# Depthwise convolution and two bias additions: from TensorE's matmuls to VectorE's passes

## The chip, the cores and the metric

The kernel runs on one core of one Trainium2 chip. The metric is the device time of one execution in microseconds (us), the median of three runs. Engines are named as in the profile: PE is TensorE's matmul and PEld its weight load, DVE is VectorE, ACT is ScalarE, POOL is GpSimd, SP is SyncE.

## The reference

Eight images of 56 x 56 positions with 128 channels, float32, go through two layers. The part that the change touches, cut to its lines:

```python
# x: [8, 56, 56, 128]
xp = x @ w_in + b_in
h = conv3x3_depthwise(x, dw_w) + dw_b            # feature_group_count = C
h = (h - bn_m) * (bn_g / sqrt(bn_v + 1e-05)) + bn_b
h = gelu(h)
offset = (h @ w_off + b_off).reshape(N, H, W, GROUP, P, 2)          # P = 9 samples
mask = softmax((h @ w_msk + b_msk).reshape(N, H, W, GROUP, P))
y = dcn_core(xp, offset, mask) @ w_out + b_out   # bilinear samples at the offsets, weighted
x = x + gamma1 * layer_norm(y, ln1_g, ln1_b)
m = gelu(x @ w_fc1 + b_fc1) @ w_fc2 + b_fc2
x = x + gamma2 * layer_norm(m, ln2_g, ln2_b)
```

Behind it comes layer 1: an additive attention (for every pair of positions the tanh of a sum of two 16-vectors, scored, exponentiated, masked to earlier positions and summed over the normalized x), then a routed feed-forward with 64 experts that each choose 8 positions of an image.

## The kernel before

An image is cut three ways: into 7 bands of 8 rows (448 positions), into 49 subs of 64 positions, and into 25 blocks of 128 positions (the last has 64). Channels or positions lie on the 128 partitions.

For each **band**, step `image_in` transposes x on PE and DVE copies it into the zero-bordered image `x_pad` (channels on partitions). `project_in` makes xp, and 27 steps `patches` write 2 x 2 patches of xp to HBM. `conv` is the depthwise convolution of the band: nine PE matmuls with the diagonal matrices `taps`, one for each tap, into the bank `side_ps`; ACT applies batch norm and gelu from `side_ps` into `h_band` (L1653). `offsets` multiplies `h_band` by the offset and mask weights (14 small matmuls, L1788), and DVE turns the result into gather indices (L1310 and what follows, about fifteen instructions); `weights` makes the corner weights after ACT's exp of the mask.

For each **sub**, POOL issues 18 indirect DMAs (L1189) that gather the patches into one of four slots of `gathered`. It may do so when DVE has finished the sub that used the slot before. DVE's step `sample` multiplies the gathered patches by the weights in six passes (L1372) and sums them into `y` (L1375). I call the 18 gathers of a sub a **burst**.

For each **block** follows the chain `turn`, `mix`, `turn_mid`, `hidden`, `mlp_out`, `turn_norm`, `keys`: PE and DVE (for `hidden` ACT) take turns on the one bank `chain_ps`. `mix` is the output projection, `mlp_out` the MLP's second layer; the biases of both are added by a matmul of a row of ones with the bias row (L1799, L1820), and both end in DVE's `add_norm`. Then the attention: ACT makes `unit` (tanh, L1677), PE `score` (L1846), ACT `exp` (L1687), PE and DVE `values` (L1746, L1441, L1875), DVE `finish`; `route` and `logits` prepare layer 1's second half. PE's matmuls of float32 stand in the trace as two records each.

**What sets the order.** Each engine runs one fixed list of steps. `list_schedule` makes it in Python when the kernel is built: from due times (`due_times`), needs (`needs`) and assumed durations (`LASTS`) it places the steps of many images until they repeat, and `order_of` gives the period that the loop over pairs of images repeats; `first_order` and `last_order` make the lists ahead of and behind the loop. An engine that waits for a semaphore therefore holds up all that stands behind in its list. All steps in `SIDE` share the one PSUM bank `side_ps`; PE begins one when the reader of the one before has signalled.

## Time and profile before

| what | value |
|---|---|
| median of three runs | 15282.85 us (15266.24 to 15287.42) |
| profiled execution, its own time | 15399.26 us |
| its span, first to last instruction | 15397.4 us |
| busy PE, PEld | 7675.1 us (50%), 3859.4 us (25%) |
| busy DVE, ACT, POOL | 5935.6 us (39%), 6773.1 us (44%), 6700.8 us (44%) |
| mean granted TensorE clock | 0.697 of full speed |

Span and time of the profiled execution differ by 1.9 us; it is 0.76% longer than the median of the plain runs. Busy shares are means over the whole span; none is near 100%, so what bounds the kernel has to be read from waits. POOL's last gather ends at 14967.99 us; ahead of it the span is eight images with one and the same rhythm, behind it the rest of the last image.

### The profile page before, as it was taken

The page shows a single profiled execution, that of the slowest core. Times are in us where ns is not written, and L with a number is a line of the kernel's source. Part 1 is how long each engine was busy: PE and PEld are TensorE (multiplying, and loading weights), DVE is VectorE, ACT ScalarE, POOL GpSimd, SP SyncE. Part 2 cuts the span into 40 slices and gives each one's busy share as a digit, 9 for nine tenths or more (in the row PEclk, how much of TensorE's full clock was granted, in tenths as well). Part 3 has the DMA queues.
Part 4 walks back from the last instruction along what each step waited for, and adds up shares of the span by engine and source line. Part 5 has one row for each costly group of instructions (what it writes and reads, how often), then busy time and mean ns, then how long its engine had stood idle before and what let it go on. Part 6 is the DMA issues. An engine that isn't in the chain of part 4 may idle for free.

```text
span 15397.4 us, 152662 instructions
## 1 busy us (share of the span) xinstructions
PE 7675.1 (50%) x45913; PEld 3859.4 (25%) x45913; DVE 5935.6 (39%) x17381; ACT 6773.1 (44%) x8210; POOL 6700.8 (44%) x7060
## 2 busy tenths in 40 slices
PE   3344554455534555445554455444654445544467
PEld 2122222222222222222222222222222222222234
DVE  3333334333343334333334333443333433343343
ACT  1234642455424554245533455334553355523455
POOL 4444444444444344444444444444444444444430
PEclk6566776677766776667766777666776677766778
DMA  2111111111111111111111111111111111212324
GB/s 61 45 46 34 31 42 44 45 33 34 40 46 41 31 36 42 47 39 32 38 40 46 39 32 37 43 46 37 31 40 41 48 35 33 57 55 62 94 69 158
DMA packets 453794, 711.94 MB, mean 46 GB/s; under 512 B 146561, under 2 KB 260994, under 8 KB 451330
## 3 DMA queue, kind: packets, MB, share of 16 engines
q0 software_dynamic: 225792, 462.87, 11.3%
q1 hardware_dynamic: 227170, 239.11, 4.9%
q8 instruction: 384, 6.29, 0.2%
q14 instruction: 448, 3.67, 0.1%
HBM read 595.45 MB, written 105.96 MB: 46 GB/s over the span
## 4 chain that ended last, share of the span: by engine, by line
another core or an unknown queue 36%; ACT 16%; PE 16%; issue 14%; DVE 12%; DVEq 5%; DMA 1%; SPq 0%; POOL 0%; ACTq 0%; POOLq 0%
ACT tanh L1677 13%; PE score_ps L1846 7%; DVEq L1208 5%; DVE pool_mem L1372 2%; PE value_ps L1875 2%; DVE newton L1243 2%; PE side_ps L1777 1%; DVE rstd L1245 1%; PE turn_ps L1746 1%; PE chain_ps L1814 1%; ACT expo L1687 1%; DVE bst L1250 1%; ACT L1687 1%; PE chain_ps L1822 1%
## 5 line engine op out<-in xcount | busy, mean ns | idle before, releaser
L1677 ACT ACTIVATE tanh<-key_rep,query 128x896 f32<-128x896 f32 (+7 forms) x6400 | 5560.0, 950 | 5834.7 <-remote 3382.9
L1189 POOL DMA_INDIRECT pool_mem<-patches_even,pool_mem x3528 | 3350.3, 950 | 4142.1 <-DVE y L1375 3038.2
L1189 POOL DMA_INDIRECT pool_mem<-patches_odd,pool_mem x3528 | 3350.3, 950 | 4124.9 <-DVE y L1375 3100.9
L1846 PE MATMUL score_ps<-tanh,score_w 128*32 128x512 f32 (+3 forms) x24320 | 3703.9, 650 | 2566.8 <-ACT tanh L1677 1562.2
L1846 PEld LDWEIGHTS score_ps<-tanh,score_w 128*32 128x32 f32 x24320 | 855.6, 126 | 4803.6 <-issue 2891.3
L1875 PE MATMUL value_ps<-values,expoT 128*128 128x129 f32 (+1 forms) x5200 | 1019.9, 346 | 301.0 <-issue 194.6
L1372 DVE TENSOR_TENSOR pool_mem<-pool_mem 128x384 f32<-128x384 f32 x2352 | 1136.1, 552 | 47.7 <-issue 45.5
L1375 DVE TENSOR_REDUCE y<-pool_mem 128x64 f32<-128x2304 f32 x392 | 1000.9, 2553 | 36.0 <-issue 6.7
L1875 PEld LDWEIGHTS value_ps<-values,expoT 128*128 128x128 f32 (+1 forms) x5200 | 898.6, 249 | 423.2 <-issue 300.9
L1441 DVE COPY expoT<-turn_ps 128x512 f32<-128x512 f32 (+4 forms) x800 | 456.9, 572 | 1214.5 <-remote 829.0
L1746 PE MATMUL turn_ps<-ident,expo 128*128 128x128 f32 (+1 forms) x2632 | 572.9, 341 | 682.6 <-DVE expoT L1441 510.4
L1687 ACT ACTIVATE expo<-score_ps,tiny 128x896 f32<-128x896 f32 (+9 forms) x416 | 383.4, 922 | 897.1 <-remote 599.8
L1243 DVE SCALAR_TENSOR_TENSOR newton<-rstd,newton 128x1 f32<-128x1 f32 (+1 forms) x2403 | 528.3, 220 | 211.4 <-issue 34.9
L1746 PEld LDWEIGHTS turn_ps<-ident,expo 128*128 128x128 f32 (+1 forms) x2632 | 393.8, 178 | 822.9 <-DVE expoT L1441 452.5
L1250 DVE BATCH_NORM_STATS2 bst<-chain_ps 128x6 f32<-128x128 f32 (+1 forms) x400 | 118.3, 296 | 1231.6 <-remote 721.2
L1814 PE MATMUL chain_ps<-chainT,w_fc 128*128 128x128 f32 (+1 forms) x1600 | 338.6, 379 | 501.1 <-DVE chainT L1394 418.8
L1687 ACT ACT_TABLE_LOAD x197 | 252.8, 1283 | 760.1 <-remote 686.3
L1831 PE MATMUL chain_ps<-chainT,w_key 128*128 128x128 f32 (+1 forms) x400 | 140.4, 450 | 843.5 <-DVE chainT L1410 563.8
L1777 PE MATMUL side_ps<-pool_mem,early 128*128 128x448 f32 x1008 | 427.5, 581 | 108.1 <-DVEq L1208 107.0
L1245 DVE SCALAR_TENSOR_TENSOR rstd<-newton,rstd 128x1 f32<-128x1 f32 (+1 forms) x2403 | 385.7, 161 | 222.0 <-issue 31.8
L1394 DVE COPY chainT<-chain_ps 128x128 f32<-128x128 f32 (+1 forms) x200 | 57.3, 287 | 1070.0 <-remote 894.4
L1814 PEld LDWEIGHTS chain_ps<-chainT,w_fc 128*128 128x128 f32 x1600 | 300.8, 280 | 599.2 <-DVE chainT L1394 459.9
(170 smaller groups left out, 6557.5 us busy)
## 6 DMA issues: line engine op xcount, KB each, us to landing
pool_mem<-in_weight SPq DMA_DIRECT2D x64, 1024.0 KB, 9.1
pool_mem<-patches_even,pool_mem POOLq DMA_INDIRECT x3528
pool_mem<-patches_odd,pool_mem POOLq DMA_INDIRECT x3528
patches_even<-pool_mem SPq DMA_DIRECT2D x104, 256.0 KB, 2.0
patches_odd<-pool_mem SPq DMA_DIRECT2D x104, 256.0 KB
pool_mem<-in_x SPq DMA_DIRECT2D x56, 224.0 KB
x_tok<-in_x SPq DMA_DIRECT2D x192, 64.0 KB
x_d<-x SPq DMA_DIRECT2D x192, 64.0 KB
```

The costliest lines, as they stand in the source:

```text
L1189: pool.indirect_dma_start(gathered[:, b, j * 4 * CG:(j + 1) * 4 * CG], None, patches_flat[int(odd)], bass.IndirectOffsetOnAxis(ap=index[:, ...
L1208: return v.drain()
L1243: v.scalar_tensor_tensor(newton[:r, 1:2], rstd[:r], rstd[:r], newton[:r, 0:1], ALU.mult, ALU.mult)
L1372: v.tensor_tensor(part, part, weight[:, lo:lo + PIECE].unsqueeze(2) .to_broadcast([P, PIECE, CG, 4]), ALU.mult)
L1375: v.tensor_reduce(y[:, i // 2 % 2, b].rearrange("p (g c) -> p g c", c=CG), product.rearrange("p (g t) c k -> p g c t k", g=2), AX_XY, ALU. ...
L1677: nc.scalar.activation(tanh[:, ui % TANH_SLOTS, :w], key_rep[:, lo:lo + w], ACT.Tanh, bias=query[:, col:col + 1]).then_inc(tanh_done.sem, 1)
L1687: nc.scalar.activation(expo[:r, ci % 2, :w], score_ps[:r, ci % 2, :w], ACT.Exp, bias=tiny[:r, 2:3])\
L1746: return mm(out, src, ident[:r, :r], is_transpose=True, start=True, stop=True)
L1777: last = mm(side_ps[:, :BAND], taps[:, t], x_pad[:, i * BAND_ROWS + dy:(i + 1) * BAND_ROWS + dy, dx:dx + W], start=t == 0, stop=t == TAPS - 1)
L1814: last = mm(chain_ps[:, c * P:c * P + r], w_fc1[:, c * P:(c + 1) * P], chainT[:, :r], start=True, stop=True)
L1846: last = mm(score_ps[32 * col:32 * col + 32, ci % 2, lo:hi], score_w[:, place], tanh[:, ui % TANH_SLOTS, lo:hi], start=place == 0, stop=pl ...
L1875: last = mm(value_ps[:r, :C + 1], expoT[:wj, pi % 2, z, :r], values[:wj, value_place(odd, j)], start=j == 0, stop=j == k)
```

## The change

VectorE makes the convolution. For each band it runs nine passes over `x_pad` shifted by the tap: the first multiplies by the tap's weight of each channel, the eight others multiply and add to `conv_sum`, a new SBUF tile. ACT reads `conv_sum` in place of `side_ps`. The diagonal matrices `taps`, PE's nine matmuls and the rule that held `side_ps` until ACT had read it are gone. In `add_norm` a DVE addition of the bias rows (now copied to all partitions by the host's `layout`) into the new tile `biased` comes first, and the two one-row matmuls are gone. The planner's `LASTS` and `needs` follow, so the order of all steps is made anew.

```diff
-FRONT = 10072
+FRONT = 10520
...
-SIDE = ("image_in", "project_in", "patches", "conv", "offsets", "route", "logits") + LATE_SIDE
-SIDE_READER = {"conv": "act"}
+SIDE = ("image_in", "project_in", "patches", "offsets", "route", "logits") + LATE_SIDE
...
-    ("pe", "image_in"): .7, ("pe", "project_in"): 1.9, ("pe", "patches"): .7, ("pe", "conv"): 9.0, ("pe", "offsets"): 1.8,
-    ("pe", "turn"): .35, ("pe", "mix"): 1.2, ("pe", "turn_mid"): .35, ("pe", "hidden"): 1.9, ("pe", "mlp_out"): 1.7,
-    ("dve", "sample"): 6.0, ("dve", "turn"): .35, ("dve", "mix"): 3.5, ("dve", "turn_mid"): .35, ("dve", "mlp_out"): 6.7,
+    ("pe", "image_in"): .7, ("pe", "project_in"): 1.9, ("pe", "patches"): .7, ("dve", "conv"): 5.7, ("pe", "offsets"): 1.8,
+    ("pe", "turn"): .35, ("pe", "mix"): .9, ("pe", "turn_mid"): .35, ("pe", "hidden"): 1.9, ("pe", "mlp_out"): 1.4,
+    ("dve", "sample"): 6.0, ("dve", "turn"): .35, ("dve", "mix"): 3.9, ("dve", "turn_mid"): .35, ("dve", "mlp_out"): 7.1,
...
-        out["pe", ("image_in", g)] = [at(0, "sp", "image_in", g), at(1, "pe", "conv", NBAND - 1)]
-        out["dve", ("image_in", g)] = [at(0, "pe", "image_in", g)]
+        out["pe", ("image_in", g)] = [at(0, "sp", "image_in", g)]
+        out["dve", ("image_in", g)] = [at(0, "pe", "image_in", g), at(1, "dve", "conv", NBAND - 1)]
-        out["pe", ("conv", g)] = [at(0, "dve", "image_in", min(g + 1, NBAND - 1)), used,
+        out["dve", ("conv", g)] = [at(0, "dve", "image_in", min(g + 1, NBAND - 1)), used, before("act", "conv", g, NBAND),
                                   before("pe", "offsets", g, NBAND)]
-        out["act", ("conv", g)] = [at(0, "pe", "conv", g)]
+        out["act", ("conv", g)] = [at(0, "dve", "conv", g)]
...
-            for t in range(TAPS):
-                v.tensor_scalar(taps[:, t], ident[:], dw[:, t:t + 1], None, ALU.mult)
...
-                moments(src, r)
-                v.scalar_tensor_tensor(ln_a[:r], src, mv[:r, 0:1], affine[:r, s], ALU.subtract, ALU.mult)
+                v.tensor_tensor(biased[:r], src, rows[:r, s // 3 * C:(s // 3 + 1) * C], ALU.add)
+                settle()
+                moments(biased[:r], r)
+                v.scalar_tensor_tensor(ln_a[:r], biased[:r], mv[:r, 0:1], affine[:r, s], ALU.subtract, ALU.mult)
...
+                elif what == "conv":
+
+                    wait(h_ready, n, i - 1)
+                    total_ = conv_sum.rearrange("p (a b) -> p a b", b=W)
+                    for t in range(TAPS):
+                        dy, dx = divmod(t, 3)
+                        tap = x_pad[:, i * BAND_ROWS + dy:(i + 1) * BAND_ROWS + dy, dx:dx + W]
+                        if t == 0:
+                            v.tensor_scalar(total_, tap, dw[:, t:t + 1], None, ALU.mult)
+                        else:
+                            v.scalar_tensor_tensor(total_, tap, dw[:, t:t + 1], total_, ALU.mult, ALU.add)
+                        last = settle()
+                    last.then_inc(conv_done.sem, 1)
...
-                    nc.scalar.activation(h_band[:], side_ps[:, :BAND], ACT.Gelu, bias=bn[:, 1:2], scale=bn[:, 0:1])\
+                    nc.scalar.activation(h_band[:], conv_sum, ACT.Gelu, bias=bn[:, 1:2], scale=bn[:, 0:1])\
...
-                elif what == "conv":
-                    side_free()
-                    wait(band_copied, n, min(i + 1, NBAND - 1))
-                    for t in range(TAPS):
-                        dy, dx = divmod(t, 3)
-                        last = mm(side_ps[:, :BAND], taps[:, t],
-                                  x_pad[:, i * BAND_ROWS + dy:(i + 1) * BAND_ROWS + dy, dx:dx + W],
-                                  start=t == 0, stop=t == TAPS - 1)
...
-                    last = mm(chain_ps[:r, :C], ones[:, :r], rows[:, :C], start=True, stop=False)
...
-                    mm(chain_ps[:r, :C], ones[:, :r], rows[:, C:], start=True, stop=False)
```

Three places show what the new order does. In each, line numbers of the kernel after are 10 higher on DVE and 4 to 7 different on PE than those of before. The first is DVE's list around the `offsets` of band 2, from the `sample` of sub 20 on. In the kernel before:

```order
L1372 TENSOR_TENSOR pool_mem<-pool_mem 128x384 x6
L1375 TENSOR_REDUCE y<-pool_mem 128x64
L1410 COPY chainT<-chain_ps 128x128
L1430 TENSOR_TENSOR expo<-expo,earlier 128x128
L1302 COPY pool_mem<-side_ps 128x512
L1417 COPY key_rep<-chain_ps 128x128
L1418 SCALAR_TENSOR_TENSOR spread<-chain_ps,tiny,own_row 128x128
L1420 TENSOR_REDUCE query<-spread 128x16
L1441 COPY expoT<-turn_ps 128x512
L1372 TENSOR_TENSOR pool_mem<-pool_mem 128x384 x6
L1375 TENSOR_REDUCE y<-pool_mem 128x64
L1310 TENSOR_TENSOR pool_mem<-side_ps,grid 128x252
```

The same place in the kernel after:

```order
L1382 TENSOR_TENSOR pool_mem<-pool_mem 128x384 x6
L1385 TENSOR_REDUCE y<-pool_mem 128x64
L1420 COPY chainT<-chain_ps 128x128
L1288 TENSOR_SCALAR pool_mem<-pool_mem,dw 128x448
L1290 SCALAR_TENSOR_TENSOR pool_mem<-pool_mem,dw 128x448 x8
L1427 COPY key_rep<-chain_ps 128x128
L1428 SCALAR_TENSOR_TENSOR spread<-chain_ps,tiny,own_row 128x128
L1430 TENSOR_REDUCE query<-spread 128x16
L1440 TENSOR_TENSOR expo<-expo,earlier 128x128
L1451 COPY expoT<-turn_ps 128x512
L1320 TENSOR_TENSOR pool_mem<-side_ps,grid 128x252
```

The convolution stands between the copies of `turn_norm` and `keys`, and `offsets` has moved ahead of the `sample` of sub 21. PE's list at the same band, before, from the transpose of `turn_norm`:

```order
L1746 MATMUL chain_ps<-ident,values 128x128
L1831 MATMUL chain_ps<-chainT,w_key 128x128
L1832 MATMUL chain_ps<-chainT,w_q 128x128
L1746 MATMUL turn_ps<-ident,expo 128x128 x4
L1777 MATMUL side_ps<-pool_mem,early 128x448 x9
L1746 MATMUL turn_ps<-ident,expo 128x128
L1875 MATMUL value_ps<-values,expoT 128x129 x4
L1846 MATMUL score_ps<-tanh,score_w 32x512 x4
L1846 MATMUL score_ps<-tanh,score_w 32x128 x4
L1788 MATMUL side_ps<-early,pool_mem 64x54 x14
```

And after:

```order
L1753 MATMUL chain_ps<-ident,values 128x128
L1841 MATMUL score_ps<-tanh,score_w 32x512 x8
L1826 MATMUL chain_ps<-chainT,w_key 128x128
L1827 MATMUL chain_ps<-chainT,w_q 128x128
L1753 MATMUL turn_ps<-ident,expo 128x128 x4
L1784 MATMUL side_ps<-early,pool_mem 64x54 x14
```

The nine long matmuls are gone, and the `offsets` matmuls follow the `keys` and one quad of transposes. The second place is DVE's list at the end of the stretch of sub 34. Before, from the copy of `turn_mid` of block 16 on:

```order
L1394 COPY chainT<-chain_ps 128x128
L1441 COPY expoT<-turn_ps 128x512 x2
L1372 TENSOR_TENSOR pool_mem<-pool_mem 128x384 x6
L1375 TENSOR_REDUCE y<-pool_mem 128x64
L1250 BN_STATS bst<-chain_ps 128x6
L1252 BN_AGGR mv<-bst 128x2
```

After:

```order
L1404 COPY chainT<-chain_ps 128x128
L1451 COPY expoT<-turn_ps 128x512 x2
L1264 TENSOR_TENSOR biased<-chain_ps,rows 128x128
L1247 BN_STATS bst<-biased 128x6
L1249 BN_AGGR mv<-bst 128x2
```

The `mlp_out` of block 16 has moved ahead of the `sample` of sub 34. In the same way that of block 24 moved from behind the `sample` of sub 1 to ahead of it, and that of block 18 the other way round, from the end of the stretch of sub 38 into that of sub 39. The third place is DVE's list at band 4, in the next stretch. Before:

```order
L1410 COPY chainT<-chain_ps 128x128
L1417 COPY key_rep<-chain_ps 128x128
L1418 SCALAR_TENSOR_TENSOR spread<-chain_ps,tiny,own_row 128x128
L1420 TENSOR_REDUCE query<-spread 128x16
L1430 TENSOR_TENSOR expo<-expo,earlier 128x128
L1310 TENSOR_TENSOR pool_mem<-side_ps,grid 128x252
```

After:

```order
L1420 COPY chainT<-chain_ps 128x128
L1288 TENSOR_SCALAR pool_mem<-pool_mem,dw 128x448
L1290 SCALAR_TENSOR_TENSOR pool_mem<-pool_mem,dw 128x448 x8
L1427 COPY key_rep<-chain_ps 128x128
L1428 SCALAR_TENSOR_TENSOR spread<-chain_ps,tiny,own_row 128x128
L1430 TENSOR_REDUCE query<-spread 128x16
L1440 TENSOR_TENSOR expo<-expo,earlier 128x128
L1451 COPY expoT<-turn_ps 128x512
L1382 TENSOR_TENSOR pool_mem<-pool_mem 128x384 x6
L1385 TENSOR_REDUCE y<-pool_mem 128x64
L1320 TENSOR_TENSOR pool_mem<-side_ps,grid 128x252
```

Here the convolution again stands behind the copy of `turn_norm`, and `offsets` has moved behind a `sample`, to the front of the next sub's stretch. The offsets of bands 0, 1 and 5 stay in the stretch in which they were; that of band 6 moved behind the `sample` of sub 0, that of band 3 ahead of the `sample` of sub 28.

## Rows read from the trace of the kernel before

**Rows 1.** Busy time of each engine in one period (window, length, PE, PEld, DVE, ACT, POOL, granted clock)

```profile
5759.00:7628.00 1869.00, 941.33 (x5433) 456.84 (x5425) 717.42 (x2130) 839.74 (x1020) 836.27 (x882) 0.70 0.14 39
```

**Rows 2.** Waits: engine, line, releaser, us in total, times, longest

```profile
POOL pool_mem L1189 <- DVE y L1375: 6139.2, 350, 43.8
ACT tanh L1677 <- remote: 3382.9, 279, 40.4
```

**Rows 3.** Timeline of POOL, the burst that begins at 6514.43 and the next

```profile
6514.43 0.95 POOL L1189 DMA_INDIRECT pool_mem<-patches_odd,pool_mem  x1 [34.12 <-DVE y L1375]
...
6518.19 1.10 POOL L1189 DMA_INDIRECT pool_mem<-patches_odd,pool_mem  x1 [0.30 <-issue]
...
6558.52 0.95 POOL L1189 DMA_INDIRECT pool_mem<-patches_odd,pool_mem  x1 [0.31 <-issue]
```

**Rows 4.** Timeline of PE beside those two bursts

```profile
6515.77 8.04 PE L1777 MATMUL side_ps<-pool_mem,early 128*128 128x448 f32 x18
...
6535.06 0.25 PE L1788 MATMUL side_ps<-early,pool_mem 128*64 128x54 f32 x1 [1.15 <-issue]
6536.46 1.01 PE L1846 MATMUL score_ps<-tanh,score_w 128*32 128x512 f32 x1 [1.15 <-issue]
...
6565.19 2.72 PE L1846 MATMUL score_ps<-tanh,score_w 128*32 128x128 f32 x18 [0.98 <-issue]
```

**Rows 5.** Timeline of DVE at band 2, same stretch

```profile
6516.94 2.93 DVE L1372 TENSOR_TENSOR pool_mem<-pool_mem 128x384 f32<-128x384 f32 x6
6519.94 2.55 DVE L1375 TENSOR_REDUCE y<-pool_mem 128x64 f32<-128x2304 f32 x1
6565.35 0.42 DVE L1310 TENSOR_TENSOR pool_mem<-side_ps,grid 128x252 f32<-128x252 f32 x1 [42.85 <-remote]
```

**Rows 6.** Timeline of DVE, then of PE, at band 0

```profile
6010.55 2.55 DVE L1375 TENSOR_REDUCE y<-pool_mem 128x64 f32<-128x2304 f32 x1
...
6038.73 0.42 DVE L1310 TENSOR_TENSOR pool_mem<-side_ps,grid 128x252 f32<-128x252 f32 x1 [18.77 <-remote]
...
6042.97 0.29 DVE L1394 COPY chainT<-chain_ps 128x128 f32<-128x128 f32 x1 [0.19 <-issue]
...
6015.94 1.03 PE L1788 MATMUL side_ps<-early,pool_mem 128*64 128x54 f32 x28
```

**Rows 7.** Timeline of PE, then of DVE, at band 4

```profile
7039.35 7.03 PE L1777 MATMUL side_ps<-pool_mem,early 128*128 128x448 f32 x18
...
7035.12 2.55 DVE L1375 TENSOR_REDUCE y<-pool_mem 128x64 f32<-128x2304 f32 x1
...
7048.49 0.29 DVE L1410 COPY chainT<-chain_ps 128x128 f32<-128x128 f32 x1 [4.03 <-remote]
7064.11 0.29 DVE L1417 COPY key_rep<-chain_ps 128x128 f32<-128x128 f32 x1 [15.33 <-remote]
```

**Rows 8.** Timeline of DVE, mlp_out of block 18 and the sample behind it

```profile
7190.41 0.30 DVE L1250 BATCH_NORM_STATS2 bst<-chain_ps 128x6 f32<-128x128 f32 x1 [2.38 <-PE chain_ps L1822]
7190.78 0.18 DVE L1252 BATCH_NORM_AGGREGATE mv<-bst 128x2 f32<-128x6 f32 x1
...
7197.13 2.90 DVE L1372 TENSOR_TENSOR pool_mem<-pool_mem 128x384 f32<-128x384 f32 x6
```

**Rows 9.** Groups of instructions by line; busy us, mean ns, idle before

```profile
L1777 PE MATMUL side_ps<-pool_mem,early 128*128 128x448 f32 x1008 | 427.5, 581 | 108.1 <-DVEq L1208 107.0 <-issue 1.1
L1799 PE MATMUL chain_ps<-rows,ones 1*128 1x128 f32 (+1 forms) x400 | 111.4, 363 | 113.3 <-issue 67.4 <-DVE chainT L1381 44.3
L1820 PE MATMUL chain_ps<-rows,ones 1*128 1x128 f32 (+1 forms) x400 | 106.2, 348 | 188.6 <-ACT hid L1663 183.0 <-issue 5.2
L1507 DVE SCALAR_TENSOR_TENSOR pool_mem<-pool_mem,early 128x448 f32<-128x448 f32 x21 | 12.8, 679 | 0.2
L1269 DVE TENSOR_TENSOR ln_b<-mid,affine 128x128 f32<-128x128 f32 x192 | 54.1, 282 | 0.1
L1310 DVE TENSOR_TENSOR pool_mem<-side_ps,grid 128x252 f32<-128x252 f32 x56 | 23.4, 418 | 730.2 <-remote 715.1 <-PE side_ps L1788 14.9
```

More of the change, by code:

```diff
@@ L459, in simulate @@
                 banks[bank_of[n, step]] = True
-        elif step[0] in SIDE and e == SIDE_READER.get(step[0], "dve"):
+        elif step[0] in SIDE and e == "dve":
             side_free = True
@@ L510, in late_steps @@
     turns, last = ROW_T // 4, len(units) - 1
-    front = [at("dve", "weights", NBAND - 1), at("pe", "conv", NBAND - 1), at("pe", "patches", NPATCH - 1),
+    front = [at("dve", "weights", NBAND - 1), at("dve", "conv", NBAND - 1), at("pe", "patches", NPATCH - 1),
              at("sp", "patches", NPATCH - 1), at("sp", "patches", NPATCH - 2), at("pe", "offsets", NBAND - 1)]
@@ L616, in first_order @@
     todo = [(n, e, s) for (e, s), t in times.items() for n in range(2) if n * period + t < period]
-    read = {(n, s) for n, e, s in todo if e == SIDE_READER.get(s[0], "dve")}
+    read = {(n, s) for n, e, s in todo if e == "dve"}
     def due_of(n, step):
@@ L708, in network @@
         dw = sb("dw", [P, TAPS])
-        early = sb("early", [P, TAPS * C + 2 + C + 2 * PARAMS + PARAMS])
+        early = sb("early", [P, 1040])
         views = Views(early)
-        taps = views.take(TAPS * C).rearrange("p (t c) -> p t c", c=C)
         bn = views.take(2)
@@ L715, in network @@
         b_par = views.take(PARAMS)
+        views_end = views.at
         w_out = sb("w_out", [P, 2, C])
@@ L718, in network @@
         w_fc2 = sb("w_fc2", [P, HID // P, C])
-        rows = sb("rows", [1, 2 * C])
+        rows = sb("rows", [P, 2 * C])
+        biased = sb("biased", [P, C])
         b_hid = sb("b_hid", [P, HID // P])
-        ones = sb("ones", [1, P])
         affine = sb("affine", [P, 6, C])
@@ L737, in network @@
         h_band = views.take(BAND)
+        conv_sum = views.take(BAND)
         xy = views.take(BAND_SUBS * SAMPLES * 2).rearrange("p (t s a) -> p t s a", s=SAMPLES, a=2)
@@ L949, in network @@
         schedule = list_schedule()
-        side_uses_of = {age: sum(a == age and step[0] in SIDE and step[0] != "conv"
+        side_uses_of = {age: sum(a == age and step[0] in SIDE
                                  for a, step in order_of("pe", schedule)) for age in (-1, 0, 1)}
-        last_conv_of_period = [(age, step[1]) for age, step in order_of("pe", schedule) if step[0] == "conv"][-1]
         block = ctx.enter_context(nc.Block())
@@ L1215, in _ @@
             v.memset(x_pad[:], 0.0)
+            v.memset(early[:, views_end:], 0.0)
             v.memset(xp_flat[:], 0.0)
-            v.memset(ones[:], 1.0)
             v.memset(y[:], 0.0)
@@ L1803, in task @@
                             last = mm(chain_ps[part, :C], chainT[part, half * SUB:(half + 1) * SUB], w_out[part, half],
-                                      start=False, stop=half == 1)
+                                      start=half == 0, stop=half == 1)
                     last.then_inc(mixed.sem, 1)
@@ L1819, in task @@
                     wait(gelu_done, n, i)
[L1820 removed]
                     for c in range(HID // P):
[L1822 removed]
+                        last = mm(chain_ps[:r, :C], hid[:, c, :r], w_fc2[:, c], start=c == 0, stop=c == HID // P - 1)
                     last.then_inc(mlp_done.sem, 1)
```

20 lines of the change are left out of this document (5 added, 15 removed).

## The prediction

> **What bounds the kernel now.** I began with the page's busy shares: no engine is above 50% of the span, so no sum of busy times is the bound. One period of an image shows the same: of 1869 us PE is busy 941, DVE 717, ACT 840 and POOL 836, at a granted clock of 0.70 [rows 1]. I went on to the waits. The longest is POOL's, 6139 us in 350 waits, for DVE's `y` [rows 2]: the gather of a sub starts when DVE has finished the sub whose slot it takes. The reader should see in it that POOL is always ready and DVE late.
>
> Then POOL's timeline. A burst is 18 gathers, and two bursts in a row reach from 6514.43 to 6559.47, 45.04 us or 22.5 each [rows 3]. 49 bursts make 1103 of the 1869 us. PE's timeline beside them is the key to the kernel. At first PE runs freely: the convolution's 18 records start 1.3 us behind the burst's start and take 8.04 us. Later its matmuls go out one by one, 1.40 us from start to start at 6535.06 and 6536.46, and only from 6565.19, 5.7 us after the last gather, does a group of 18 go in 2.72 us [rows 4]. What PE has done also reaches DVE late: at band 0 the 28 records of `offsets` end at 6016.97, and DVE takes them at 6038.73, 25.6 us after its `sample` ended at 6013.10 [rows 6]. At band 2, with two bursts in a row, it waits 42.85 us [rows 5]. ACT's tanh loses 3383 us to such "remote" releases [rows 2].
>
> So the rhythm of a sub is: `sample` ends, the burst starts, a few microseconds in which PE, DVE and ACT pass work on, a freeze, the release at about +26 (at band 4 `sample` ends at 7037.67 and DVE gets on at 7064.11, 26.4 later [rows 7]), the work that the release frees, the next `sample` of 5.5 us (6516.94 to 6522.49) [rows 5]. 49 times 26 us is 1274 of 1869; the other 595 us, 12.1 for a sub, are `sample` and 6.6 us of other DVE work and waits. My rule for every edit follows: **DVE work ahead of the release costs nothing until it fills the 26 us; DVE work behind the release costs its whole length, since the next burst waits for it.**
>
> **The change part by part.** *The convolution leaves PE.* 1008 records and 427.5 us go, 7.6 us for each of 56 bands [rows 9]. No step of DVE waits for them but through `offsets`, and those wait for the release in any case: L1310 loses 715 us to remote releases, 12.8 for a band, and 14.9 us in all to PE's matmuls as such [rows 9]. I credit nothing directly. What it may give is PE time in the open window at a burst's start, at most 8 us a band; that is a rival below.
>
> *It comes to DVE.* Eight SCALAR_TENSOR_TENSORs of 128x448 at 0.679 us, a row of the same operation and size [rows 9], are 5.4; the TENSOR_SCALAR ahead lies between 0.3 (as an operation of 128 elements) and 0.68, I take 0.5; nine gaps of 0.08, as between the first two instructions of an `add_norm` [rows 8], are 0.7. Together 6.65 us, 372 for 56 bands. At band 2 and band 4 it stands directly behind the copy of `turn_norm`, at the other bands behind a `sample`, a `turn` or an `mlp_out` in the first half of the stretch. At band 4 that copy came at 7048.49, and the next one, `keys`, was frozen until 7064.11 [rows 7]: 15.33 us of wait cover the 6.65. The same cover is there at band 2 (42.85) [rows 5] and band 0 (18.77) [rows 6]. Cost nothing; without the cover 6.65 us for each band that loses it, 53 us for a band of eight images. Bounds: 0 and 372.
>
> *It lies beside the gathers.* The six passes of a `sample` fall into a burst at 6516.94 to 6519.87, and two or so of the 18 gathers took 1.10 in place of 0.95 us [rows 3, 5]. These six passes have two SBUF operands, like the eight new ones, and take 2.93 us. So I take 0.3 us for a band, 17 us in all; bounds 0 and, if every gather beside a pass stood still for it, 5.9 us for a band.
>
> The Trainium skill, page "SBUF — State Buffer", section "Who interferes with whom", speaks against the change here: a VectorE operation with two SBUF inputs and GpSimd share one port pair, as an exclusive lock that the first to start holds for its whole instruction. By that rule the gathers would stand still for most of the 5.9 us of a band, against the 0.3 that the row suggests; the sum would be some 300 us worse.
>
> *The biases.* 800 records and 217.6 us leave PE [rows 9]; for 400 steps DVE gets an addition of 0.28 us, by the same form in L1269 [rows 9], and a gap of 0.08: 0.36. In a chain the two nearly cancel: two records at 0.36 overlap to about 0.4. But where the matmuls lay in the freeze, or the step waits only for the release, PE's part was free and DVE's is not. I take a fifth of the 400, 80 times 0.36 less what the rest gives back: +10, bounds −40 and +70.
>
> *The new order.* Steps moved ahead of the release gain their length, steps moved behind it lose it. An `offsets` is 4.24 us on DVE (6038.73 to 6042.97) [rows 6]; an `mlp_out` 6.72 (7190.41 to 7197.13) [rows 8]. A `sample` that comes early makes two bursts stand back to back.
> - Band 2: before, one wait of 42.85 and then `offsets` and the chain. Now `offsets` stands ahead of `sample` 21 and waits for the release of its own burst, then a second release: 26.4+4.2+5.5+26.4 = 62.5, in place of 8.8 for the short stretch (from 0.8 ahead of the burst at 6514.43 to 6522.49) +42.9+4.2 = 55.9; but the `weights` and `mix` that came behind, some 3.5 each, and a copy or two, go under the second freeze, 11 in all. Together −4.5.
> - Band 3: in the same way, `offsets` now stands in the stretch whose release it waits for, and the `weights` and `mlp_out` behind it come partly under the next freeze, less the conversion of a short stretch into a full one; I take −3.
> - `mlp_out` of block 18 goes from behind a release to ahead of one: −6.7, and its wait of 2.4 with it [rows 8], less 1.5 for the copies that come in: −7.5.
> - `mlp_out` of blocks 16 and 24 goes the other way, +7.1 each with the bias and up to 2 of waiting; band 4's `offsets` goes under cover, −4.2, and so does band 6's with what stood beside it, −8. Together +3.
> - Bands 0, 1, 5: same place, frozen before and after: 0.
>
> −12 us an image; −84 for seven, as the first begins differently. The first stretches get three convolutions and three `offsets` among the patches; I take +10 for the prologue (bounds −20, +50).
>
> **Sum:** −84 +17 +10 +10 = −47. The profiled execution took 15399.26 us, its span is 1.9 less, so a profiled run of the new kernel would take 15352. It was 0.76% over the median of the plain runs, 15282.85; the same 47 us off that gives 15236, say 15235.
>
> **The rivals.**
> - *The cadence stands* (15283, within 15255 to 15310): the moves of the order cancel, since each stretch is a freeze plus one chain and the planner only shuffles which. For it: five of my terms are 3 to 8 us with either sign. Against: the `mlp_out` of block 18 is plainly moved out.
> - *PE's window opens* (about 15000): the 7.6 us that PE gets back at a burst's start let a score group or a chain step through before the freeze. If one `mlp_out` or two small handoffs more a band get ahead, 5 us, that is 5 x 56 = 280. For it: at bands 2 and 4 the convolution ran 8.04 and 7.03 us right there [rows 4, 7]. Against: PE is not the one that DVE finds slow there.
> - *Slower: the nine passes close DVE's window.* In the first 8 us of a burst the chain passes from DVE to PE and back. Where the convolution stands ahead of a `turn` or `keys` copy, 6.65 us late is after the freeze began, so the next step (a `mix`, half an `mlp_out` and the bias, about 3.9) is done behind the release instead of ahead. Four bands of an image: 4 x 3.9 x 8 = 125, with the rest of the sum 15360; with three of the convolutions themselves behind a release, 160 more, 15520. For it: at band 3 and 5 the convolution comes at the front. Against: at band 4 the next copy was frozen anyway [rows 7]. It decides from two bands on, when it eats the 47.
> - *The lock*: gathers stand still beside the passes, 5.4 us a band, 56 x 5.4 = 300 more: 15535. Against it: the six passes of `sample` cost 0.3 [rows 3, 5].
>
> **How the numbers follow.** Plain runs spread by 0.14%, so 0.2%, 31 us, is about what can be told from no change: faster is under 15252, slower over 15313. Forecast 0.40, its own range 15130 to 15300, 0.34 of it in faster; cadence stands 0.16; window opens 0.14; window closed 0.24; lock 0.06. Faster 0.48, same 0.22, slower 0.30. Leaving out 0.05 below and the upper end of the closed window and the lock above gives 15000 to 15450.
>
> **What the changed profile would show.** DVE busy up by about 500 us, PE down by about 640. The STT of L1290 at 0.68 us; longer if gathers hold it. A burst with a convolution in it 22.5 long, not 28. DVE's copies behind the convolution still "remote", ending about 26 us behind a `sample`. `y` of POOL's waits at about 6090 us; if it grows by over 100, the window closed. A `sample` of band 2 with two separate waits of some 20 us in place of 42.85. The prediction is wrong if the freeze no longer starts where it did, or if the convolution is found behind a release.

## The result, and the profile after

The kernel after takes 15209.3 us (median of five runs, 15191.58 to 15225.52), the kernel before 15287.4 in the same comparison: a ratio of 0.9949, 95% interval 0.9936 to 0.9963. That is 78 us less, where 47 were forecast. Of the five series of runs, the three in the middle ran on chips where the kernel behaves in another way; that became the main finding, below.

The profiled execution of the kernel after has a span of 15209.5 us. First the windows of one period of an image (columns as in [rows 1]):

```profile
5710.00:7558.00 1848.00, 839.80 (x5239) 404.34 (x5231) 774.51 (x2257) 852.59 (x1030) 849.38 (x885) 0.69 0.14 40
```

PE has lost 102 us of work in it and DVE gained 57, POOL's gathers have grown by some 10 (885 of them fall into this window, 882 into the other), and the window is 21 us shorter than in [rows 1]. The waits of the kernel after, beside [rows 2]:

```profile
POOL pool_mem L1188 <- DVE y L1385: 5838.7, 324, 45.6
ACT tanh L1687 <- remote: 3667.0, 295, 37.8
```

POOL waits 300 us less for `y`, where some 50 were expected; part of it is the profiled execution of before, which was 112 us above its median. The groups that answer to [rows 9]:

```profile
L1290 DVE SCALAR_TENSOR_TENSOR pool_mem<-pool_mem,dw 128x448 f32<-128x448 f32 x448 | 306.5, 684 | 34.9 <-issue 1.3
L1264 DVE TENSOR_TENSOR biased<-chain_ps,rows 128x128 f32<-128x128 f32 x384 | 110.8, 289 | 1018.8 <-remote 669.9 <-PE chain_ps L1799 196.4 <-PE chain_ps L1817 110.7
L1288 DVE TENSOR_SCALAR pool_mem<-pool_mem,dw 128x448 f32<-128x448 f32 x56 | 25.2, 451 | 1.8
L1320 DVE TENSOR_TENSOR pool_mem<-side_ps,grid 128x252 f32<-128x252 f32 x56 | 23.4, 417 | 256.8 <-remote 246.6 <-PE side_ps L1784 9.1
```

The prices of the instructions came out: 0.684, 0.451 and 0.289 us against 0.679, 0.5 and 0.282. What I had not seen is in the last line. DVE waited 730 us ahead of the 56 `offsets` before [rows 9], and waits 257 now. Most of it went at band 2, from 49 to 4.5 us a wait in the mean of the eight images. DVE's timeline there, beside [rows 5]:

```profile
6452.82 2.55 DVE L1385 TENSOR_REDUCE y<-pool_mem 128x64 f32<-128x2304 f32 x1
...
6455.48 0.45 DVE L1288 TENSOR_SCALAR pool_mem<-pool_mem,dw 128x448 f32<-128x448 f32 x1
6456.01 6.00 DVE L1290 SCALAR_TENSOR_TENSOR pool_mem<-pool_mem,dw 128x448 f32<-128x448 f32 x8
...
6470.80 0.42 DVE L1320 TENSOR_TENSOR pool_mem<-side_ps,grid 128x252 f32<-128x252 f32 x1 [5.31 <-remote]
...
6475.74 2.90 DVE L1382 TENSOR_TENSOR pool_mem<-pool_mem 128x384 f32<-128x384 f32 x6 [0.54 <-issue]
...
6507.87 0.29 DVE L1391 COPY chainT<-chain_ps 128x128 f32<-128x128 f32 x1 [15.73 <-PE chain_ps L1753]
```

And PE's, beside [rows 4]:

```profile
6463.68 1.09 PE L1753 MATMUL turn_ps<-ident,expo 128*128 128x128 f32 x4 [6.83 <-issue]
6464.69 1.75 PE L1784 MATMUL side_ps<-early,pool_mem 128*64 128x54 f32 x28
...
6466.64 1.93 PE L1870 MATMUL value_ps<-values,expoT 128*128 128x129 f32 x8
6468.50 3.98 PE L1841 MATMUL score_ps<-tanh,score_w 128*32 128x512 f32 x25
6473.61 0.27 PE L1841 MATMUL score_ps<-tanh,score_w 128*32 128x128 f32 x1 [1.13 <-issue]
```

The 28 records of `offsets` go out in one go, 8.5 us into the burst, and DVE has them at 6470.80. Before, 19 of them went out by 6526.55 and the last nine crept out until 6535.06 [rows 4]; DVE had them only after 42.85 us of wait. PE is not slowed before 6473.6, 17 us into this burst; in the one of before it was after 12. So the open window has no fixed length in time.

I counted PE's records (matmuls and weight loads) from each burst's start to the point where they begin to go out one by one, taken as five pauses in a row of 0.7, 1.4 or 2.1 us between records. At 115 such points of before the middle half lies between 113 and 131 records, but between 11 and 17 us; at 102 of after between 118 and 144 records, and 12 and 18 us. Handoffs from PE to DVE close earlier, but sort in the same way. Of those at `turn_mid` in the first 20 us behind a burst's start (of two bursts in a row, the first one's), DVE saw 73 more than 10 us late in before, and all but one of these had 74 records or more ahead of them; the 12 that it saw within 4 us had 46 or fewer. In after the 58 late ones had 70 or more, the 14 prompt ones 76 or fewer, though some of the prompt ones came as late as 16 us and the late ones as early as 6. **The window is nearer to a number of instructions than to a time.** This is read from the traces; no experiment changed that number where the freeze occurs.

PE's windows at the two bursts of [rows 4] show the same step (length, PE's busy time and its matmuls, granted clock, then the DMA engines' busy share and GB/s; the first is the open window, the last the stretch behind the release):

```profile
6513.00:6526.00 13.00, 12.10 (x53) 0.81 0.22 62
6526.00:6563.00 37.00, 11.80 (x43) 0.58 0.18 50
6563.00:6576.00 13.00, 11.02 (x77) 0.63 0.05 20
```

At band 2 the convolution's 18 matmul records with their 18 loads took over a quarter of such a window; now they are not there.

At band 1 it was something else. The matmul of `turn_mid` and DVE's copy of it, in before and then in after:

```profile
6254.51 0.33 PE L1746 MATMUL chain_ps<-ident,mid 128*128 128x128 f32 x1 [2.57 <-issue]
6272.60 0.29 DVE L1394 COPY chainT<-chain_ps 128x128 f32<-128x128 f32 x1 [17.61 <-remote]
```

```profile
6213.20 0.47 PE L1753 MATMUL chain_ps<-ident,mid 128*128 128x128 f32 x1 [7.65 <-DVE mid L1398]
6213.88 0.29 DVE L1404 COPY chainT<-chain_ps 128x128 f32<-128x128 f32 x1 [0.20 <-issue]
```

In before it stands 7.4 us and 84 of PE's records behind the burst's start (6247.1) and is seen 17.8 us later; in after 12 us and 76 records (start 6201.3), and is seen after 0.2. Images 1 to 6 are alike: 84 records and 17 us late in all six of before, 76 and 0.2 in all six of after. The band's convolution is no part of that, since in before its matmuls stood behind the release, 30 us into the burst. The four matmuls fewer, eight records with their loads, are two of the bias and two of `values`. That these eight carried the handoff through is my reading, and untested.

So a whole release falls away there. The first burst's `sample` comes early and two bursts stand in a row. DVE freezes too, when it has much to do in a burst: in the second one its small operations go out 1.40 us apart:

```profile
6217.45 2.56 DVE L1385 TENSOR_REDUCE y<-pool_mem 128x64 f32<-128x2304 f32 x1
...
6241.23 0.18 DVE L1249 BATCH_NORM_AGGREGATE mv<-bst 128x2 f32<-128x6 f32 x1 [1.07 <-issue]
6242.63 0.15 DVE L1235 TENSOR_SCALAR newton<-mv 128x1 f32<-128x1 f32 x1 [1.22 <-issue]
6244.03 0.15 DVE L1237 TENSOR_SCALAR rstd<-newton 128x1 int32<-128x1 int32 x1 [1.25 <-issue]
...
6253.72 0.42 DVE L1320 TENSOR_TENSOR pool_mem<-side_ps,grid 128x252 f32<-128x252 f32 x1
```

At band 0 the passes have lost their cover. In image 4, counted from 0, they stand 21 us behind the `sample`, and the next copy does not wait for a release any more:

```profile
7781.96 2.55 DVE L1385 TENSOR_REDUCE y<-pool_mem 128x64 f32<-128x2304 f32 x1
...
7805.16 0.29 DVE L1420 COPY chainT<-chain_ps 128x128 f32<-128x128 f32 x1 [7.17 <-remote]
7805.37 0.47 DVE L1288 TENSOR_SCALAR pool_mem<-pool_mem,dw 128x448 f32<-128x448 f32 x1
7805.91 6.00 DVE L1290 SCALAR_TENSOR_TENSOR pool_mem<-pool_mem,dw 128x448 f32<-128x448 f32 x8
7812.11 0.29 DVE L1427 COPY key_rep<-chain_ps 128x128 f32<-128x128 f32 x1 [0.20 <-issue]
```

In images 1 to 6 they begin 22, 21, 13, 21, 18 and 17 us behind the `sample`, and DVE waits only 0.8 to 3.8 us between them and the next `sample`. That stretch takes 40.6, 39.1, 33.9, 39.1, 38.0 and 37.8 us, in place of 33.2, 37.0, 34.2, 33.2, 33.1 and 37.1: 3.5 more in the mean, and nothing more in image 3, where they begin early. At the other bands the passes are covered, by DVE's later waits (bands 2, 3, 5 and 6, 6.5 us and more) or by a burst that is longer than the stretch (bands 1 and 4, stretches of 19 and 16 us beside bursts of 22).

Last POOL at band 2. Before, two gathers of a burst were 0.15 longer [rows 3]. Now the four beside the passes take 1.36 and three times 1.21 us:

```profile
6456.15 1.36 POOL L1188 DMA_INDIRECT pool_mem<-patches_odd,pool_mem  x1 [36.05 <-DVE y L1385]
6457.82 1.21 POOL L1188 DMA_INDIRECT pool_mem<-patches_odd,pool_mem  x1 [0.30 <-issue]
...
6460.85 1.21 POOL L1188 DMA_INDIRECT pool_mem<-patches_odd,pool_mem  x1 [0.30 <-issue]
```

### The profile page after: what moved, and what is told of

It reads as the page before. It is cut to its first block, busy times and chain, and to the rows that moved or that the text cites. A ratio compares the mean times of both kernels' runs of the same rounds, so it can differ in the third digit from the quotient of the medians.

```text
span 15209.5 us, 150958 instructions
## 1 busy us (share of the span) xinstructions
PE 7036.1 (46%) x44105; PEld 3476.1 (23%) x44105; DVE 6371.3 (42%) x18276; ACT 6815.7 (45%) x8238; POOL 6773.1 (45%) x7060
## 4 chain that ended last, share of the span: by engine, by line
another core or an unknown queue 35%; ACT 18%; DVE 14%; issue 14%; PE 11%; DVEq 6%; DMA 1%; SPq 0%; ACTq 0%
ACT tanh L1687 15%; PE score_ps L1841 5%; DVEq L1207 5%; DVE pool_mem L1382 2%; DVE newton L1240 2%; DVE rstd L1242 1%; DVE pool_mem L1290 1%; PE value_ps L1870 1%; PE chain_ps L1810 1%; DVE bst L1247 1%; PE turn_ps L1753 1%; ACT expo L1697 1%; ACT L1673 1%; DVE mv L1249 1%
## 5 line engine op out<-in xcount | busy, mean ns | idle before, releaser
L1188 POOL DMA_INDIRECT pool_mem<-patches_even,pool_mem x3528 | 3388.3, 960 | 4005.7 <-DVE y L1385 2874.2
L1188 POOL DMA_INDIRECT pool_mem<-patches_odd,pool_mem x3528 | 3384.5, 959 | 3997.1 <-DVE y L1385 2964.6
L1870 PE MATMUL value_ps<-values,expoT 128*128 128x129 f32 (+1 forms) x5200 | 982.6, 340 | 322.7 <-issue 193.9
L1870 PEld LDWEIGHTS value_ps<-values,expoT 128*128 128x128 f32 (+1 forms) x5200 | 867.7, 243 | 428.9 <-issue 277.5
L1264 DVE TENSOR_TENSOR biased<-chain_ps,rows 128x128 f32<-128x128 f32 (+1 forms) x400 | 115.3, 288 | 1031.5 <-remote 669.9
L1391 DVE COPY chainT<-chain_ps 128x128 f32<-128x128 f32 x200 | 57.9, 290 | 1108.2 <-remote 642.9
L1753 PE MATMUL chain_ps<-ident,values 128*128 128x128 f32 (+1 forms) x200 | 82.0, 410 | 746.7 <-issue 433.7
```

Source lines behind the costliest of these rows:

```text
L1188: pool.indirect_dma_start(gathered[:, b, j * 4 * CG:(j + 1) * 4 * CG], None, patches_flat[int(odd)], bass.IndirectOffsetOnAxis(ap=index[:, ...
L1753: return mm(out, src, ident[:r, :r], is_transpose=True, start=True, stop=True)
L1870: last = mm(value_ps[:r, :C + 1], expoT[:wj, pi % 2, z, :r], values[:wj, value_place(odd, j)], start=j == 0, stop=j == k)
```

## The experiments

### Biases and order apart (first chip)

The planner's durations set the order, so two kernels with the same `LASTS` have the same order of steps. That gives pairs that differ in the work alone.

`e1_before_new_costs`, the kernel before with

```diff
-    ("pe", "mix"): 1.2, ("pe", "mlp_out"): 1.7, ("dve", "mix"): 3.5, ("dve", "mlp_out"): 6.7
+    ("pe", "mix"): .9, ("pe", "mlp_out"): 1.4, ("dve", "mix"): 3.9, ("dve", "mlp_out"): 7.1
```

> The kernel before with the planner's assumed durations of mix and mlp_out as in the kernel after (0.9, 1.4 on PE, 3.9, 7.1 on DVE); the work is unchanged, only the order of steps is made anew. Theory (a new order by itself moves the time, since steps cross the release): a ratio to before away from 1, between 0.993 and 1.007. Rival (the order's details cancel): within 0.1% of before.

`e2_biases_on_dve`, the same durations and also

```diff
-                moments(src, r)
+                v.tensor_tensor(biased[:r], src, rows[:r, s // 3 * C:(s // 3 + 1) * C], ALU.add)
+                settle()
+                moments(biased[:r], r)
...
-                    mm(chain_ps[:r, :C], ones[:, :r], rows[:, C:], start=True, stop=False)
```

> Only the biases move to VectorE, the convolution stays on PE; the order is that of the run before this one, so the two differ in the biases alone. Theory: the bias additions cost about what they give, +10 us (from -40 to +70) against e1_before_new_costs. Rival (two records of PE leave every chain and this is the gain of the change): 60 us or more faster than e1_before_new_costs.

`e3_after_old_costs`, the kernel after with the first diff reversed:

> The kernel after with the planner's assumed durations of mix and mlp_out as in the kernel before; the work is that of the kernel after, the order another one. Theory: another order of the same work, ratio to before 0.990 to 1.000, so that it differs from the kernel after (0.9949) by some tenths of a per cent. Rival: the same 0.995 within 0.1%.

`e4_conv_on_dve`, that and the second diff reversed, so that only the convolution is on DVE:

> Only the convolution moves to VectorE, the biases stay on PE as one-row matmuls; its order is that of e3_after_old_costs, so the two differ in the biases alone. Theory: within 40 us of e3_after_old_costs, faster by some 10 us. Rival (the biases' PE time is the gain): 60 us or more slower than e3_after_old_costs.

The surprise was the base: on this chip the kernel before takes 9429.6 us (median of 21 runs), not 15287. Against it:

| run | median, us | ratio, 95% interval |
|---|---|---|
| e1_before_new_costs | 9433.7 | 1.0004 (0.9995 to 1.0013) |
| e2_biases_on_dve | 9434.9 | 1.0006 (0.9997 to 1.0015) |
| e3_after_old_costs | 9501.2 | 1.0074 (1.0060 to 1.0088) |
| e4_conv_on_dve | 9499.5 | 1.0075 (1.0061 to 1.0088) |

On this chip the biases are worth nothing either way: +1.3 us (e2 against e1) and +1.6 us (e3 against e4), within the spread. The convolution on DVE, with the order that it brings, costs 70 us (e4), where e3 had been expected at 0.990 to 1.000. The new order alone is worth nothing in e1, as the rival had it. The waits of POOL in e1 say what differs from the chip of the prediction:

```profile
POOL pool_mem L1189 <- issue: 2142.5, 7029, 0.3
POOL pool_mem L1189 <- DVEq L1208: 72.6, 1, 72.6
POOL pool_mem L1189 <- DVE y L1375: 7.9, 26, 0.3
```

POOL waits for `y` 7.9 us, not 6139 [rows 2]. From 73 us on the 392 bursts follow each other with nothing but 0.3 us between gathers, so POOL is the bound and everything else lies beside it. PE beside the gathers is not frozen: the search that found 115 points in before finds one in this trace, and none in e5, e8 and e10. The granted clock is 0.83 over the span, not 0.70. On such a chip a kernel gains only by shorter gathers, an earlier first one, or less behind the last.

### What the eight passes cost (second chip)

`e5_after_again` is the kernel after, unchanged. `e6_one_pass` and `e7_seventeen_passes` change the loop of the convolution and keep the order; e6 leaves out eight taps, e7 adds them twice:

```diff
-                    for t in range(TAPS):
+                    for t in range(1):                             # e6_one_pass
+                    for t in (*range(TAPS), *range(1, TAPS)):      # e7_seventeen_passes
```

`e8_pe_one_matmul` is the kernel before with PE's loop cut to one tap.

> The kernel after, unchanged, so that the other three have their base on the same chip. Where the kernel before takes about 9430 us (gathers end to end, POOL is the bound): ratio 1.007, as POOL starts some 30 us later and its bursts grow by 55 us. Where before takes about 15280 us (PE frozen beside gathers): 0.995 again.

> The kernel after with one of the nine passes: the TENSOR_SCALAR stays, the eight passes that multiply and add are left out, the order is kept. Theory (the two-operand passes hold up the gathers beside them): where before takes about 9430 us, POOL's bursts shrink by nearly all of the 55 us and the prologue by 15, so 60 to 75 us faster than the kernel after, back at before or 5 us under it. Rival (the order made anew moves POOL's chain, the passes are hidden): within 15 us of the kernel after. Where before takes about 15280 us: theory (passes lie in the freeze) within 60 us of after; rival (they push handoffs behind the release) 120 us or more faster.

> The kernel after with the eight multiply-and-add passes made twice (17 passes for a band; the sum is another one), the order is kept. Theory: where before takes about 9430 us, another 1.0 us for each of 56 bands and 16 in the prologue, 60 to 80 us slower than the kernel after. Rival (port held as a full lock from now on): 5 us a band, 280 or more slower. Where before takes about 15280 us: theory 0 to 100 slower, rival (no cover) 300 slower.

> The kernel before with one of the nine matmuls of the convolution (eight taps left out), the order is kept: PE's relief without anything on DVE. Theory: where before takes about 9430 us POOL is the bound and PE's 6.8 us a band are free, within 10 us of before. Rival (PE's relief is a gain of its own): 100 us or more faster. Where before takes about 15280 us: theory (open window used by others) 0 to 150 faster; rival: no change at all.

Here too before takes 9420.0 us, and POOL is the bound:

| run | median, us | ratio, 95% interval | first gather at | sum of 392 bursts |
|---|---|---|---|---|
| e5_after_again | 9518.9 | 1.0103 (1.0087 to 1.0118) | 102.1 | 8918.1 |
| e6_one_pass | 9451.7 | 1.0031 (1.0020 to 1.0043) | 85.0 | 8874.7 |
| e7_seventeen_passes | 9592.4 | 1.0182 (1.0168 to 1.0196) | 119.8 | 8970.1 |
| e8_pe_one_matmul | 9414.2 | 0.9994 (0.9985 to 1.0003) | 68.7 | 8845.4 |

Eight passes fewer save 67 us, eight more cost 74: close to a straight line. In the traces 17 to 18 of it lie in the prologue (first gather 17.1 earlier, 17.7 later), 43 and 52 in the bursts, or 0.8 to 0.9 us for each of 56 bands. PE's relief alone is worth nothing (e8). The theory's 1.0 us a band holds, the rival's 5 us do not. But e6 was to be back at before, and is 32 us slower: the passes are two thirds of what the change costs here. Against e8 its first gather comes 16 us later and its bursts are 29 us longer, 21 of them in a few very long gathers that the next series explains in part. The kernel after had been expected at 1.007 and is at 1.010.

### Which passes hold a gather, and is the order free (third chip)

`e9_one_operand` replaces the nine passes by thirteen with one operand in SBUF, so the convolution is left out and DVE stays as busy:

```diff
-                    for t in range(TAPS):
+                    for t in (*range(TAPS), *range(4)):
...
-                        if t == 0:
+                        if True:
                             v.tensor_scalar(total_, tap, dw[:, t:t + 1], None, ALU.mult)
```

> The kernel after with thirteen TENSOR_SCALAR passes (one SBUF operand each, 0.445 us) in place of the one and eight; nothing is accumulated, so the convolution is left out, but DVE is busy as long (13 x 0.53 = 6.8 us a band) and the order is kept. Theory (gathers wait for passes with two SBUF operands): where before takes about 9430 us, about as e6_one_pass in the bursts (sum of the 392 bursts near 8880 us, not 8918), the prologue as long as in the kernel after, so 45 to 55 us faster than the kernel after. Rival (any long DVE pass beside a gather holds it): within 10 us of the kernel after. Where before takes about 15280 us: bursts with a convolution in them 23.0 us long in place of 24.1, and the time 0 to 70 us under the kernel after.

`e10_after_third` is the kernel after, `e11_after_old_costs` the one of e3.

> The kernel after, unchanged, as the base of this call. Where before takes about 9430 us: ratio 1.010 as in e5_after_again, if that was no matter of the chip; 0.995 where before takes about 15280 us.

> The kernel of e3_after_old_costs beside the kernel after on one chip: same work, another order. Where before takes about 9430 us: theory (POOL is the bound, the order is free) within 0.1% of e10_after_third; rival (the 1.0074 of e3 against the 1.0103 of e5 is the order): 0.3% faster. Where before takes about 15280 us: theory (the order sets which work lies behind the release) 0.3% or more apart; rival: within 0.1%.

Before takes 9419.0 us. e9 takes 9469.0 (1.0053, 1.0040 to 1.0067), e10 9518.5 (1.0104, 1.0088 to 1.0119), e11 9493.9 (1.0078, 1.0064 to 1.0092). e9 is 49 us under e10, as the theory had it. POOL and DVE of e10 at one convolution:

```profile
4141.91 0.95 POOL L1188 DMA_INDIRECT pool_mem<-patches_odd,pool_mem  x1 [0.30 <-issue]
4143.17 1.21 POOL L1188 DMA_INDIRECT pool_mem<-patches_odd,pool_mem  x1 [0.30 <-issue]
4144.68 1.22 POOL L1188 DMA_INDIRECT pool_mem<-patches_odd,pool_mem  x1 [0.30 <-issue]
...
4141.36 6.00 DVE L1290 SCALAR_TENSOR_TENSOR pool_mem<-pool_mem,dw 128x448 f32<-128x448 f32 x8
```

The same in e9, where thirteen passes fill 7.75 us:

```profile
4119.19 0.94 POOL L1188 DMA_INDIRECT pool_mem<-patches_odd,pool_mem  x1 [0.30 <-issue]
...
4121.68 0.95 POOL L1188 DMA_INDIRECT pool_mem<-patches_odd,pool_mem  x1 [0.30 <-issue]
...
4118.11 7.75 DVE L1288 TENSOR_SCALAR pool_mem<-pool_mem,dw 128x448 f32<-128x448 f32 x13
```

Of the operations compared here only those with two operands in SBUF hold a gather. Over the whole trace of e10, 242 gathers overlap L1290 by more than 0.3 us and are 46 us longer in all, 0.19 each; the longest that lies wholly beside it takes 1.30 us, 0.36 more than the median. In e9, 350 overlap L1288 and are 0.6 us longer in all. A third case is in every trace: `sample`'s TENSOR_REDUCE has one operand, and of the 477 gathers of e10 wholly beside it none takes more than 0.96 us. The Trainium skill, page "SBUF — State Buffer", section "Who interferes with whom", names the right kind of operation, two SBUF inputs, though only against a GpSimd instruction that reads SBUF; on the length the measurement decides: not the whole of the passes, 0.19 us a gather.

A wait through several passes does occur, but at another place, found in the question why e11 is 24.6 us faster than e10 with the same work. In e10 eight gathers last over 1.5 us, seven of them one image apart; in e11 there are two. POOL and DVE of e5 at one of them:

```profile
4681.25 3.23 POOL L1188 DMA_INDIRECT pool_mem<-patches_even,pool_mem  x1 [0.30 <-issue]
...
4680.52 0.47 DVE L1414 TENSOR_SCALAR values<-x,mv,rstd 64x128 f32<-64x128 f32 x1
4680.78 2.89 DVE L1382 TENSOR_TENSOR pool_mem<-pool_mem 128x384 f32<-128x384 f32 x6
```

A `sample` follows the `mlp_out` of block 24 without a gap, and the gather does not end before its six passes are over. Of the 392 `sample`s of e10, 128 begin before the operation ahead of them has ended, and all eight long gathers lie beside these; none lies beside the 264 others. So in this trace no gather is held that long without the missing gap, but the missing gap alone does not do it. These gathers cost e10 18 us and e11 2, and the bursts of e10 are 10.5 us longer in all; the tail behind the last gather gives the rest (383 and 369 us). So the rival on e11 is right: the order is not free even where POOL is the bound.

### A drain behind `mlp_out` (fourth chip)

```diff
                         .then_inc(norm_ready.sem, 1)
+                    settle()
```

> The kernel after with one more drain on DVE, behind the last instruction of mlp_out (L1414), so that the six passes of a sample never follow it directly. In the kernel after one gather of an image lasts 2.6 to 3.6 us in place of 0.95 where a sample follows the mlp_out of block 24 without a drain. Theory (the pass that is taken up without a gap holds the gather through all six): these long gathers go, 15 to 20 us of 9518, a ratio near 1.0085, less 0.08 us for each mlp_out where DVE is waited for. Rival (they come from the place in the order, whatever stands between): they stay, ratio 1.010. Where before takes about 15280 us: within 0.1% of the kernel after by either.

`settle()` issues a drain: behind it the next DVE operation starts some 0.08 us after the last one's end, while without it the `sample` above started 0.21 us before that end. Here the kernel before takes 15385.5 us (median of 14 runs, 15352 to 15433): this chip freezes as the one of the prediction did (it may be the same; the medians of before are 0.64% apart). e12 takes 15445.8, a ratio of 1.0036 (1.0024 to 1.0048), where 0.9949 within 0.1% was expected by either theory. What it was to settle, the long gather, stays open, since that hardly occurs with the freeze (one in the trace of after, one here). But its trace shows the slower side of the forecast. DVE at band 0 of image 3, from the copy of `turn_norm`, in the kernel after and then in e12, where the burst ended at 6043.2:

```profile
5953.15 0.29 DVE L1420 COPY chainT<-chain_ps 128x128 f32<-128x128 f32 x1 [5.35 <-remote]
5953.36 0.45 DVE L1288 TENSOR_SCALAR pool_mem<-pool_mem,dw 128x448 f32<-128x448 f32 x1
5953.88 5.99 DVE L1290 SCALAR_TENSOR_TENSOR pool_mem<-pool_mem,dw 128x448 f32<-128x448 f32 x8
```

```profile
6040.93 0.29 DVE L1421 COPY chainT<-chain_ps 128x128 f32<-128x128 f32 x1 [9.24 <-remote]
6041.14 0.44 DVE L1288 TENSOR_SCALAR pool_mem<-pool_mem,dw 128x448 f32<-128x448 f32 x1
6041.66 5.99 DVE L1290 SCALAR_TENSOR_TENSOR pool_mem<-pool_mem,dw 128x448 f32<-128x448 f32 x8
```

In the kernel after the passes run from 13 to 20 us behind the `sample`, in e12 from 21 to 28, across the release, and that stretch is 39.2 us long in place of 33.9. Image 3 is the one in which the two differ most there: over images 1 to 6 the stretch takes 41.8 us in e12 and 38.1 in the kernel after. All of e12's images are 33 us longer in the mean; the ten stretches of subs 4 to 13 hold 11 of it, the rest is spread over the period. Whether one drain of 0.08 us brings that about, or the place and time of the series do (before is 0.64% slower there as well), I can't tell: the kernel after wasn't run beside it.

## Why the prediction was right, and where it was not

The time was right: 15235 forecast, 15209 measured, inside the likeliest case's own range. The main step held in the main: 332 us of passes and 115 of bias additions came to DVE, and at six of seven bands the passes are covered. At band 0 they are not, by 3.5 us an image. By the prediction's own two signs of being wrong, the freeze that no longer starts where it did (band 2: 17 us into the burst, not 12) and a convolution behind a release (band 0), its mechanism was wrong in part. The terms fared less well than the sum. Stretches between `sample`s, mean of images 1 to 7, from the two profiled executions (that of before was 0.73% above its median of 15287.4, 14 us an image; the last column has it scaled down by that):

| term | forecast, us an image | as measured | scaled |
|---|---|---|---|
| band 2 (subs 20 to 22) | −4.5 | +0.4 | +1.3 |
| band 3 (28 to 30) | −3 | −5.9 | −5.0 |
| `mlp_out` of block 18 (37 to 39) | −7.5 | −9.5 | −8.6 |
| blocks 16 and 24, bands 4 and 6 (0 to 3, 34 to 36) | +3 | +15.9 | +18.0 |
| band 1 (14, 15) | 0 | −15.7 | −15.2 |
| band 5 (42, 43) | 0 | +6.7 | +7.2 |
| all other stretches, band 0 among them | 0 | −18 | −10.5 |
| sum | −12 | −26 | −13 |

The sum of −13 beside the −12 forecast is luck: four rows are off by 7 to 15 us and nearly cancel. The whole adds up as well: seven images give −90, which holds the growth of gathers and the biases too, image 0 +1 and the part behind the last `sample` +10, which no term had; together −79, where the medians differ by 78.

- **"Bands 0, 1, 5: same place, frozen before and after: 0"** is the step that failed. It took the freeze to begin at a place in the list and at a time, which the traces do not bear out. At band 1 `turn_mid` got through with 76 of PE's records ahead of it in place of 84, and a whole release fell away; at band 0 the passes ran into the release, +3.5; band 5 has +7.2, and I did not find its cause. The rival "PE's window opens" is there at band 2, where the convolution's 36 records were; at band 1 the convolution was not in the window, and its 280 us are not there.
- Band 2: the mechanism is another one than I gave. `offsets` did not wait for the release, and the two waits of some 20 us that I expected are one of 5 and one of 16 (for `turn`). Stretches 21 and 22 take 28 and 48 us where they took 10 and 66, so that the sum is as before.
- **"I take 0.3 us for a band, 17 us in all"**: the sum of the bursts grew from 8732.5 to 8804.7, 72 us, 1.3 a band. The size of the hold was read from a burst where only two gathers were longer (and with them the price of a hold, 0.15 us in place of 0.24); the eight passes of a band meet four gathers, at 0.24 each (218 gathers, 51.6 us), and the gathers beside `sample` grew by 13 us more. The lock's 5.4 us a band are not there. The Trainium skill, page "SBUF — State Buffer", section "Who interferes with whom", sets two SBUF inputs only against a GpSimd instruction that reads SBUF, a condition that the prediction left out.
- The prologue: +10 forecast; image 0 ended 13 us earlier, which the scaling turns into +1, though the first gather began 27.5 us later (101.9, not 74.4). DVE's two longest waits for `offsets` there are 15 and 42 us in place of 12 and 93.
- The biases: +10 forecast, nothing measured in e1 to e4, on a chip where POOL is the bound. What they are worth with the freeze was not measured; band 1 is where they may have given something.
- What no step asked: whether the freeze belongs to the kernel. It belongs to the chip or its state: the kernel before takes 15287 and 15385 us in two series and 9419 to 9430 in three, and the traces of the kernel after show it in the first series and not in e5 and e10. With it the change gives 0.51% (0.37 to 0.64%), without it it costs 1.03% on two chips.

No version beats both kernels. With the freeze the kernel after is the best that ran; without it the kernel before, and e8 shows that even PE with one of nine taps gives nothing there.

What stays open: why two series freeze and three do not, and what it is that fills up (all times here are from executions of which a span and a clock were recorded, so whether the records themselves play a part can't be told either); whether the 0.9% between the kernel after and e12, each against the base of its chip, is the drain's or the series'; and how the passes would count with the freeze, since e6, e7 and e9 all ran without it; and what, besides the missing gap, makes a gather wait through a `sample`'s passes.

## What to carry to other kernels

Ask what bounds a kernel on more than one chip before moving work: here the same instructions were bound by handoffs beside the gathers on one and by the gathers themselves on another, and the change had opposite signs. The passes with two SBUF operands lengthened GpSimd's gathers by 0.19 to 0.24 us each; where gathers are the bound, count them. In a list scheduler, change the costs and the work apart: pairs with one order settled what the biases were worth where POOL is the bound. And look at every image before calling a step covered: in one of six, band 0 had kept its cover.

## What the runs showed of the hardware that I had not expected

- Two kinds of chip for one kernel: 9419 to 9430 us on three, 15287 and 15385 in the two other series. On the slow ones PE's matmuls, and sometimes DVE's operations, go out 1.40 us apart beside indirect gathers, after some 113 to 144 of PE's records. Handoffs from PE with 70 to 80 records or more ahead of them are seen only about 26 us behind the `sample`. The gathers themselves are as fast (0.95 us) on both.
- A TENSOR_SCALAR of 128x448 beside a gather holds it by 0.002 us on average (350 gathers), a SCALAR_TENSOR_TENSOR of that size by 0.19 to 0.24. Beside six TENSOR_TENSORs that follow another operation without a gap, eight gathers of e10 took 1.7 to 2.7 us longer; the other 120 such places have none.
